# Layer 2's products stream the sum of mask and degree diagonal from one 16-bit tile

## Chip, core and metric

The kernel runs on one core of a Trainium2 chip. The metric is the device time of one execution in microseconds (us). TensorE (PE) multiplies matrices into PSUM, VectorE (DVE), ScalarE (ACT) and GpSimd (POOL) do the elementwise work, and SyncE issues the DMAs. The engines run on their own and are ordered by semaphores; each works through its own list of instructions in order.

## What is computed

Four graph layers with a residual and a layer norm each, on `x` (8 batches, 2048 nodes, 64 features) and a sparse, row-normalised adjacency matrix. The change concerns layer 2:

```python
adj_i = adj + jnp.eye(N, dtype=adj.dtype)
deg = jnp.sum(adj_i, axis=1, keepdims=True)
emb = jnp.einsum('bnf,hf->bnh', x, W) + b
agg = jnp.einsum('ij,bjh->bih', adj_i, emb) / deg
x = _layernorm(x + agg, axis=-1)
```

Every row of `adj` holds one value, 1 over its number of neighbours, so the kernel keeps `adj` as a 0/1 mask and scales rows afterwards. `adj + I` is then the mask plus a diagonal of the degrees, up to a scale of the rows.

## The kernel before

**Data.** `Bm` is the mask, transposed, in 8 bits, entries 0 or 64: 16 row tiles t of 128 nodes, 2048 columns. `dg` holds for each t a 128 x 128 tile in 16 bits with 64 times the degrees on its diagonal. `S` holds the activations as two 16-bit halves (high h = 0, low h = 1) for each t and each chunk c (two of the eight batches, 128 columns, c = 0 to 3). `stile(h, t, c)` is one 128 x 128 tile of it, the stationary operand of a matmul.

**The products of layer 2.** P0 to P15, with k = 4c + j: chunk c, output columns 512j to 512j + 511 (`block(j)`). `quarter` (L791, the matmuls are at L795) does four row tiles of a product, 8 matmuls of 512 columns; four quarters make 32. Behind the last quarter come 8 matmuls of 128 columns (L945) with `dg` as the streamed operand, for the four row tiles t = 4j to 4j + 3 whose nodes are those of the block. All 40 add into one PSUM bank; the last increments `s_p`. ACT then writes the high half of the result (step `E`, L1075) and DVE the low half (L1231), to free the bank.

```python
e.wait_ge(s_sl, 4 * c + q + 1)
quarter(e, o, c, j, q, False)
if q < 3:
    continue
for i in range(4):
    t = 4 * j + i
    for h in range(2):
        m = e.matmul(o[:, 128 * i:128 * i + 128], stile(h, t, c), dg[:, t, :], ...)
```

**Order.** The order of all steps is written out by hand in `middle_order` and `last_order`, the same list for every engine; each engine does its part of each step. P0 lies between the last steps `Z` of layer 0 (L925). `last_order` begins behind the last `Z`: a key y of `late` is a place in it, and P1's first half stands behind the keys up to 2, its second half behind key 3, P2's first half behind key 4, and so on. What stands at key 0, `sum(3)` among it, comes from `middle_order`.

The other steps that matter:

- `add` (POOL): joins the parts of a `Z` step into `X`. The last is that of the last `Z`.
- `chk` (ACT): counts a row tile of the mask, with `T3[:, 0:1024]` as its junk output; sixteen of them, the last behind the last `Z`.
- `bt` (POOL, L1773): an 8-bit addition over 512 columns, 64 of them, for mask combinations that layer 3 wants from about 670 us on.
- `sum(3)` (POOL): three additions for layer 1's mean over chunk 3, behind DVE's norm of layer 0 for that chunk (L1543).
- `split(c, j)` (ACT, POOL): writes the halves `S` of layer 1's result; `s_sl` counts them. A product of chunk c waits for them.
- `W(c, j)` (PE, L780 to L782, 12 matmuls of 128 columns; DVE, four additions into `X`): the product with the weights. Needs `E` of its product and a free PSUM bank.
- `rows` (DVE): constants of layer 3. `ovr` and `sgn` (ACT): two passes over a row tile of the adjacency, a check of the inputs.
- `v0`, `D`, `G`, `M`, `cut`, `mix`: layer 3. Its products `M` (L962) begin behind P15. The cuts `S1` and `S2` write `SUM`, whose first half lies in `T3[:, 0:1024]`.

Of the kernel before, what the change touches and what calls it, by code (L numbers as in the profile page):

```python
# [6 lines left out]
F16 = mybir.dt.float16  # L7
# [7 lines left out]
NT = 16  # L15
# [166 lines left out]
def last_order(after):  # L182
# [9 lines left out]
    def on(h, *steps):  # L192
        half.setdefault(h, []).extend(steps)

    for k in sorted(after):
        at(int(2 * k), *after[k])
    for c in range(NC):
# [110 lines left out]
def gnn_kernel(nc, x_in, at_in, a_in, embt_in, sm_in, bx_in, w0_in, a12_in, w0bb_in, out):  # L308
    ctx = ExitStack()
    with ctx:  # L310
# [72 lines left out]
        s_g, s_ut, s_uh, s_ul = (sem(f"s_{k}") for k in ("g", "ut", "uh", "ul"))  # L383
        s_gt, s_gh, s_gl = (sem(f"s_{k}") for k in ("gt", "gh", "gl"))
        s_f, s_y3 = sem("s_f"), sem("s_y3")
        s_bt = sem("s_bt")
        s_mx = sem("s_mx")
        s_over = sem("s_over")
        s_t2 = sem("s_t2")
# [60 lines left out]
        rowt = WZ[:, :, :, :].rearrange("p h k n -> p (h k n)")[:, 0:4096].bitcast(F32)  # L450
        junk = WZ[:, :, :, :].rearrange("p h k n -> p (h k n)")[:, 4096:6144]
        junk_counts = T3[:, 0:1024].bitcast(F16)
        RT = [flatR[:, 512 * k:512 * k + 512] for k in range(4)]
        UT = [flatR[:, 2048 + 512 * k:2560 + 512 * k] for k in range(4)]

# [332 lines left out]
            e.matmul(o, hat[:, 0, kd, :], T[:, c, 1, block(j)], start=False, stop=False, skip_group_check=on)  # L788
            return e.matmul(o, hat[:, 1, kd, :], T[:, c, 0, block(j)], start=False, stop=True, skip_group_check=on)  # L789

        def quarter(e, o, c, j, q, last=True):  # L791

            for t in range(4 * q, 4 * q + 4):
                for h in range(2):
                    m = e.matmul(o, stile(h, t, c), Bm[:, t, block(j)], start=(t == 0 and h == 0),  # L795
                                 stop=(last and t == NT - 1 and h == 1))
            return m

        def product1(e, v, q):
# [91 lines left out]
        def tensor_steps(e, steps):  # L891
            for step in steps:
                kind = step[0]
                if kind == "P1":
                    product1(e, *step[1:])
                elif kind == "dx":
                    pe_dx(e, step)
                elif kind == "t1":
                    pe_t1(e, step)
                elif kind == "P2":  # L900
                    product2(e, *step[1:])
                elif kind == "Z":
                    u, t = step[1:]
                    c, j = divmod(u, 4)
                    n4 = 4 * u + t
                    e.wait_ge(s_dx, u + 1)
                    e.wait_ge(s_u2, u + 1)
                    e.wait_ge(s_wlo, 1)
                    k0 = slice(128 * (4 * j + t), 128 * (4 * j + t) + 128)
                    halves = ([DX[:, c % 2, h, k0] for h in range(2)], [T[:, c, h, k0] for h in range(2)],  # L910
                              [U2[:, u % 3, h, 128 * t:128 * t + 128] for h in range(2)])
                    for g in range(2):
                        n = 2 * n4 + g
                        b0 = z_bank(n)
                        if n < 3:
                            for b in (b0, b0 + 1):
                                e.wait_ge(*z_first[b])
                        else:
                            e.wait_ge(s_za, 3 * (n - 2))
                        for i in range(9):  # L920
                            kd, part = divmod(i, 3)
                            zh, wh = ((0, 0), (0, 1), (1, 0))[part]
                            for q in range(2):
                                r = slice(64 * q, 64 * q + 64)
                                m = e.matmul(bank(b0 + q), halves[kd][zh][r, :], WZ[r, wh, kd, block(g)],  # L925
                                             start=(i == 0), stop=(i == 8))
                        m.then_inc(s_zp, 1)
                elif kind == "mean":
                    o = pe_aux(e, step)
                    e.wait_ge(s_sum, step[1] + 1)  # L930
                    e.matmul(o, ones[:, :], XS, start=True, stop=True).then_inc(s_mean, 1)
                elif kind == "P":
                    k, q = step[1:]
                    c, j = divmod(k, 4)
                    o = bank(product_bank(k))
                    if q == 0:
                        e.wait_ge(*product_free(k))
                    e.wait_ge(s_sl, 4 * c + q + 1)
                    quarter(e, o, c, j, q, False)
                    if q < 3:  # L940
                        continue
                    for i in range(4):
                        t = 4 * j + i
                        for h in range(2):
                            m = e.matmul(o[:, 128 * i:128 * i + 128], stile(h, t, c), dg[:, t, :], start=False,  # L945
                                         stop=(i == 3 and h == 1))
                    m.then_inc(s_p, 1)
                elif kind == "M":
                    n, s, q = step[1:]
                    jj = q // 2  # L950
                    what, by = SLOTS[s]
                    o, b = bank(pair_bank(n, s, jj)), mask(by, jj)
                    if q % 2 == 0:
                        e.wait_ge(*pair_free[step])
                    if n == 2 and by[0] == "T":
                        e.wait_ge(s_bt, NT * (1 + BT_ORDER.index(by)))
                    if jj == 0:
                        e.wait_ge(s_ul, CN["cut", n, q, what] + 1)
                    last = s in (1, 5, 6)
                    for t in range(4):  # L960
                        for h in range(2):
                            m = e.matmul(o, half_of(n, what, h, q % 2)[:, t, :], b[:, 4 * (q % 2) + t, :],  # L962
                                         start=(s in (0, 1, 3) and q % 2 == 0 and t == 0 and h == 0),
                                         stop=(not last and q % 2 == 1 and t == 3 and h == 1), skip_group_check=s not in (0, 1, 3))
                    if q % 2 == 1:
                        if last:
                            m = beside(e, o, *ending(n, s, jj), min(n // 2 - 1, 1), on=s > 1)
                        m.then_inc(s_p, 1)
                elif kind == "t22":
                    n, jj = step[1:]  # L970
                    beside(e, pe_aux(e, step), *ending(n, 4, jj), min(n // 2 - 1, 1), True).then_inc(s_t2, 1)
                elif kind == "total":
                    o = pe_aux(e, step)
                    e.wait_ge(s_cw, 1)
                    e.matmul(o[:, 0:2], ones[:, :], sums[:, 0, :], start=True, stop=True).then_inc(s_tot, 1)
                elif kind == "W":
                    c, j = step[1:]
                    o = pe_aux(e, step)
                    e.wait_ge(s_zl, 4 * c + j + 1)
                    e.wait_ge(s_hl, 1)  # L980
                    by_weight(e, o, c, j, 5).then_inc(s_w, 1)
                elif kind == "D":
                    c, j = step[1:]
                    o = pe_aux(e, step)
                    e.wait_ge(s_vl, 4 * c + j + 1)
                    by_diagonal(e, o, c, j).then_inc(s_d, 1)
                elif kind == "G":
                    p, c, j = step[1:]
                    o = pe_aux(e, step)
                    if p == 1:  # L990
                        e.wait_ge(s_hl, 3)
                        e.wait_ge(s_dl, 4 * c + j + 1)
                    else:
                        e.wait_ge(s_gl, place(p - 1, c, j) + 1)
                    by_weight(e, o, c, j, 2 + min(p - 1, 1)).then_inc(s_g, 1)
                elif kind == "F":
                    c, j = step[1:]
                    o = pe_aux(e, step)
                    e.wait_ge(s_gl, place(3, c, j) + 1)
                    by_weight(e, o, c, j, 4).then_inc(s_f, 1)  # L1000
# [72 lines left out]
        def scalar_steps(e, steps):  # L1073
# [3 lines left out]
            for step in steps:  # L1077
# [91 lines left out]
                elif kind == "cut":  # L1169
# [3 lines left out]
                    else:  # L1173
                        e.wait_ge(s_mx, MN["mix", n, jj, what] + 1)

                    if what in ("S1", "S2", "S3"):
                        if n > 2:
                            e.wait_ge(s_p, slot_done(n - 1, {"S2": 2, "S1": 3, "S3": 4}[what], 1))
                    elif n >= 4:
                        e.wait_ge(s_p, slot_done(n - 2, [x[0] for x in SLOTS].index(what), 1))  # L1180
                    else:
                        c, j = block_of(n, jj, "X21" if what == "S4" else what)
                        e.wait_ge(s_d, 4 * c + j + 1)
# [563 lines left out]
        def gpsimd_steps(e, steps, pc):  # L1747
# [3 lines left out]
            for step in steps:  # L1751
# [22 lines left out]
                elif kind == "add":  # L1774
# [12 lines left out]
                    e.wait_ge(s_acc[1], 5 * n4 + 5)  # L1787
                    add(v, v, Y[n4 % 3]).then_inc(s_add, 1)
                    e.wait_ge(s_add, n4 + 1)
                elif kind == "sum":  # L1790
                    c = step[1]
                    e.wait_ge(s_n[0], 4 * c + 2)
# [481 lines left out]
```

## Time and profile before

| | us |
|---|---|
| median of 3 runs | 1030.81 |
| lowest, highest run | 1030.46, 1031.53 |
| span of the profiled execution | 1029.5 |
| PE busy | 1009.6 (98%) |
| DVE busy | 678.8 (66%) |
| POOL busy | 553.4 (54%) |
| ACT busy | 457.4 (44%) |
| P0's last matmul to M's first | 519 to 654.6 |

The span runs from the first to the last instruction of the profiled execution. Times in the views count from its start. Matmuls overlap: one is shown for 0.38 us (512 columns) while they start 0.22 us apart, so the spacing of starts tells their cost. A busy time of PE is no proof of full speed.

### The profile page before, as it was taken

To read this page: it belongs to the slowest core of one execution; us is meant where nothing else is said; L and a number is where in the kernel's file an instruction comes from. 1 tells how busy PE (TensorE), PEld (TensorE's weight loads), DVE (VectorE), ACT (ScalarE), POOL (GpSimd) and SP (SyncE) were. 2 spreads that over 40 slices of the span, in tenths; PEclk is the share of its full clock that TensorE was granted. 3 is DMA by queue.
4 is the path that set the end of the run, shared out by engine and by line. 5 is a ranking of instruction groups with operands and counts; after the bars stand their busy time and mean duration, and the time that the engine had idled before them with its cause. 6 is when DMAs were issued, how large, how long until landed. Compare 5 with 4: busy or idle time off the path is not lost.

```text
span 1029.5 us, 18650 instructions
## 1 busy us (share of the span) xinstructions
PE 1009.6 (98%) x6854; PEld 485.6 (47%) x6854; DVE 678.8 (66%) x1683; ACT 457.4 (44%) x1109; POOL 553.4 (54%) x645
## 2 busy tenths in 40 slices
PE   7999999999999999999999999999999999999995
PEld 3445444444444444434445556555555545455553
DVE  3886565666566786578567767886663646657556
ACT  4632323453345445543543454432556655232632
POOL 0004487776658698879878465474534233323311
PEclk9999999999999999999999999999999999999998
DMA  9930000000000000000010111000033231000022
GB/s 375 402 136 1 1 1 2 1 2 1 1 1 2 1 2 2 1 2 1 1 42 1 41 42 42 2 1 1 3 122 108 98 123 42 4 2 21 21 62 62
DMA packets 14658, 45.65 MB, mean 44 GB/s; under 512 B 960, under 2 KB 9280, under 8 KB 10080
## 3 DMA queue, kind: packets, MB, share of 16 engines
q1 hardware_dynamic: 14560, 44.39, 11.7%
q8 instruction: 56, 0.92, 0.4%
q14 instruction: 42, 0.34, 0.1%
HBM read 40.19 MB, written 4.19 MB: 43 GB/s over the span
## 4 chain that ended last, share of the span: by engine, by line
PE 90%; DVE 6%; ACT 2%; issue 1%; POOL 0%; DMA 0%; SPq 0%; ACTq 0%; DVEq 0%; POOLq 0%
PE PS L962 28%; PE PS L925 23%; PE PS L795 22%; PE PS L847 5%; PE PS L780 2%; PE PS L781 2%; PE PS L782 2%; ACT WZ L1075 1%; DVE X L1543 1%; DVE X L1231 1%; PE PS L789 1%; PE PS L787 1%; PE PS L788 1%; DVE T L1231 1%; PE PS L770 1%
## 5 line engine op out<-in xcount | busy, mean ns | idle before, releaser
L795 PE MATMUL PS<-BW,S 128*128 128x512 fp8e4 x1280 | 290.7, 379 | 0.7 <-DVE R L1231 0.7
L1075 ACT ACTIVATE T<-PS,SM 128x128 f32<-128x128 f32 x384 | 113.2, 366 | 203.8 <-DVE X L1231 135.8
L925 PE MATMUL PS<-WZ,R 64*128 64x512 f16 x1536 | 197.8, 377 | 0.0
L795 PEld LDWEIGHTS PS<-BW,S 128*128 128x128 f16 x1280 | 120.2, 98 | 149.4 <-issue 16.6
L962 PE MATMUL PS<-BW,S 128*128 128x512 fp8e4 x768 | 173.1, 379 | 0.1
L1749 POOL TENSOR_TENSOR T<-T 128x128 f32<-128x128 f32 (+1 forms) x192 | 124.3, 647 | 79.8 <-ACT T L1075 61.8
L1231 DVE SCALAR_TENSOR_TENSOR X<-PS,SM,X 128x128 f32<-128x128 f32 x320 | 109.9, 344 | 76.0 <-PE PS L925 75.9
L925 PEld LDWEIGHTS PS<-WZ,R 64*128 64x128 f16 x1536 | 69.5, 94 | 102.6 <-issue 26.3
L962 PEld LDWEIGHTS PS<-BW,S 128*128 128x128 f16 x768 | 73.8, 98 | 83.4 <-issue 0.6
L962 PE MATMUL PS<-BW,T 128*128 128x512 fp8e4 x480 | 109.3, 379 | 0.0
L1749 POOL TENSOR_TENSOR S<-R,S 128x512 f16<-128x512 f32 (+1 forms) x46 | 52.5, 1148 | 103.9 <-ACT S L1075 103.9
L1231 DVE SCALAR_TENSOR_TENSOR T<-PS,SM,T 128x128 f32<-128x128 f32 x256 | 88.1, 344 | 24.9 <-PE PS L925 24.7
L925 PE MATMUL PS<-WZ,T 64*128 64x512 f16 x768 | 103.8, 376 | 0.0
L1749 POOL TENSOR_TENSOR T<-R,T 128x512 f16<-128x512 f32 x40 | 50.4, 1269 | 84.0 <-ACT T L1075 50.3
L1075 ACT ACTIVATE WZ<-WZ,ra 128x2048 f16<-128x2048 f32 (+1 forms) x32 | 63.9, 1996 | 41.8 <-DMA WZ<-a_in 41.7
L1231 DVE SCALAR_TENSOR_TENSOR R<-PS,cs,R 128x512 f32<-128x512 f32 x48 | 36.0, 750 | 64.9 <-PE PS L789 29.2
L1773 POOL TENSOR_TENSOR BW<-BW 128x512 fp8e4<-128x512 fp8e4 x64 | 70.9, 1113 | 2.7
L962 PEld LDWEIGHTS PS<-BW,T 128*128 128x128 f16 x480 | 46.3, 98 | 52.9
L1231 DVE SCALAR_TENSOR_TENSOR R<-PS,ra,R 128x128 f32<-128x128 f32 x176 | 48.6, 343 | 30.5 <-PE PS L782 17.5
L1749 POOL TENSOR_TENSOR X<-X,T 128x128 f32<-128x128 f32 x128 | 58.5, 457 | 10.0
L780 PE MATMUL PS<-hat,T 128*128 128x128 f16 x320 | 57.1, 219 | 3.4 <-DVE T L1231 2.5
L847 PE MATMUL PS<-BW,S 128*128 128x512 fp8e4 x240 | 54.8, 393 | 5.6 <-DVE BW L1228 5.6
(210 smaller groups left out, 1496.6 us busy)
## 6 DMA issues: line engine op xcount, KB each, us to landing
WZ<-a_in SPq DMA_DIRECT2D x16, 1024.0 KB, 4.8
BW<-at_in SPq DMA_DIRECT2D x8, 1024.0 KB, 18.9
R<-at_in SPq DMA_DIRECT2D x7, 1024.0 KB, 12.9
out<-X SPq DMA_DIRECT2D x16, 256.0 KB, 2.3
X<-x_in SPq DMA_DIRECT2D x3, 1024.0 KB, 20.6
T<-w_in SPq DMA_DIRECT2D x1, 1536.0 KB, 16.1
R<-at_in SPq DMA_DIRECT2D x2, 512.0 KB, 4.1
SM<-sm_in SPq DMA_DIRECT2D x1, 520.5 KB, 18.9
```

The source lines that it names most:

```text
L770: e.matmul(o[:, 128 * k:128 * k + 128], stile(0, t, c), dg[:, t, :], start=True, stop=False)
L780: e.matmul(ok, th, hat[:, 0, kind, :], start=True, stop=False)
L781: e.matmul(ok, tl, hat[:, 0, kind, :], start=False, stop=False)
L782: m = e.matmul(ok, th, hat[:, 1, kind, :], start=False, stop=True)
L795: m = e.matmul(o, stile(h, t, c), Bm[:, t, block(j)], start=(t == 0 and h == 0), stop=(last and t == NT - 1 and h == 1))
L847: e.matmul(bank(2 * c + j), stile(h, jt, c), Bm[:, jt, block(j)], start=(jt == 0 and h == 0), stop=False)
L925: m = e.matmul(bank(b0 + q), halves[kd][zh][r, :], WZ[r, wh, kd, block(g)], start=(i == 0), stop=(i == 8))
L962: m = e.matmul(o, half_of(n, what, h, q % 2)[:, t, :], b[:, 4 * (q % 2) + t, :], start=(s in (0, 1, 3) and q % 2 == 0 and t == 0 and h == ...
L1075: return e.activation(o, i, f, **kw)
L1231: return e.scalar_tensor_tensor(out=o, in0=a, scalar=s, in1=b, op0=f, op1=g)
L1749: return e.tensor_tensor(o, a, b, f)
L1773: e.tensor_tensor(o, a, b, f, saturate=False).then_inc(s_bt, 1)
```

## The change

The mask's diagonal 128 x 128 tiles and the tiles of `dg` are added into `dm`, 16 tiles of 128 x 128 in 16 bits, which lie in `T3[:, 0:1024]`. POOL does this in four new steps `dm` of four additions each, at keys 0, 2, 4 and 6 of `last_order`, for blocks 1, 2, 3 and 0. P1 to P15 no longer have matmuls against `dg`. Their own four row tiles are done last, by `own_rows`: around each diagonal tile the columns left and right of it come from the mask, the diagonal tile from `dm`. The other twelve row tiles go in the three quarters before. P0 is left as it was. PE waits for `s_dm` ahead of the own rows, and ACT waits for `s_p` ahead of the first `S1` cuts, which overwrite `dm`.

```diff
+    for y, b in ((0, 1), (2, 2), (4, 3), (6, 0)):
+        at(y, ("dm", b))
     for k in sorted(after):
         at(int(2 * k), *after[k])
...
+        DM_AT = (0, 2, 3, 1)
+        dm = T3[:, 0:1024].bitcast(F16).rearrange("p (b i n) -> p b i n", b=4, n=128)
...
-        def quarter(e, o, c, j, q, last=True):
+        def quarter(e, o, c, j, q, last=True, first=0):
...
-                    m = e.matmul(o, stile(h, t, c), Bm[:, t, block(j)], start=(t == 0 and h == 0),
+                    m = e.matmul(o, stile(h, t, c), Bm[:, t, block(j)], start=(t == first and h == 0),
...
+        def own_rows(e, o, c, j):
+
+            for i in range(4):
+                t, d = 4 * j + i, 128 * i
+                for h in range(2):
+                    last = i == 3 and h == 1
+                    if d:
+                        e.matmul(o[:, 0:d], stile(h, t, c), Bm[:, t, 512 * j:512 * j + d], start=False, stop=False)
+                    if d < 384:
+                        e.matmul(o[:, d + 128:512], stile(h, t, c), Bm[:, t, 512 * j + d + 128:512 * j + 512],
+                                 start=False, stop=False)
+                    m = e.matmul(o[:, d:d + 128], stile(h, t, c), dm[:, DM_AT[j], i, :], start=False, stop=last)
             return m
...
-                    e.wait_ge(s_sl, 4 * c + q + 1)
-                    quarter(e, o, c, j, q, False)
+                    if k == 0:
+                        e.wait_ge(s_sl, q + 1)
+                        quarter(e, o, c, j, q, False)
...
+                    others = [x for x in range(4) if x != j]
                     if q < 3:
+                        e.wait_ge(s_sl, 4 * c + others[q] + 1)
+                        quarter(e, o, c, j, others[q], False, 4 * others[0])
                         continue
...
+                    e.wait_ge(s_sl, 4 * c + j + 1)
+                    e.wait_ge(s_dm, (4, 1, 2, 3)[j])
+                    own_rows(e, o, c, j).then_inc(s_p, 1)
...
+                    if what == "S1" and n == 2:
+
+                        e.wait_ge(s_p, 14 + 2 * jj)
...
+                elif kind == "dm":
+                    b = step[1]
+                    e.wait_ge(s_cnt, NT)
+                    e.wait_ge(s_dg, NT)
+                    for i in range(4):
+                        t = 4 * b + i
+                        m = add(dm[:, DM_AT[b], i, :], dg[:, t, :], Bm[:, t, 128 * t:128 * t + 128])
+                    m.then_inc(s_dm, 1)
```

## Rows read from the trace of the kernel before

**Rows 1.** The page, the chain that ended last, as shares of the span.
```profile
PE 90%; DVE 6%; ACT 2%; issue 1%; POOL 0%; DMA 0%; SPq 0%; ACTq 0%; DVEq 0%; POOLq 0%
```

**Rows 2.** PE's groups by line, 523 to 654 us: count, busy, mean ns, idle before.
```profile
L795 PE MATMUL PS<-BW,S 128*128 128x512 fp8e4 x480 | 106.7, 379 | 0.0
L780 PE MATMUL PS<-hat,T 128*128 128x128 f16 x89 | 15.8, 219 | 0.9 <-DVE X L1231 0.9
```

**Rows 3.** PE's instructions in order of time, 523 to 607: start, duration, what.
```profile
523.27 7.08 PE L795 MATMUL PS<-BW,S 128*128 128x512 fp8e4 x32
530.19 0.61 PE L945 MATMUL PS<-dg,S 128*128 128x128 f16 x8
530.64 7.07 PE L795 MATMUL PS<-BW,S 128*128 128x512 fp8e4 x32
...
537.99 0.22 PE L780 MATMUL PS<-hat,T 128*128 128x128 f16 x1
...
538.66 7.07 PE L795 MATMUL PS<-BW,S 128*128 128x512 fp8e4 x32
...
606.61 0.23 PE L780 MATMUL PS<-hat,T 128*128 128x128 f16 x1 [0.90 <-DVE X L1231]
```

**Rows 4.** POOL's instructions in order of time, 529 to 560: start, duration, what.
```profile
529.04 1.10 POOL L1773 TENSOR_TENSOR BW<-BW 128x512 fp8e4<-128x512 fp8e4 x1
533.86 1.64 POOL L1749 TENSOR_TENSOR SM<-X 128x512 f32<-128x512 f32 x1 [3.72 <-DVE X L1543]
535.58 2.94 POOL L1749 TENSOR_TENSOR SM<-SM,X 128x512 f32<-128x512 f32 x2
...
559.36 1.21 POOL L1749 TENSOR_TENSOR S<-X,S 128x512 f16<-128x512 f32 x1 [2.18 <-ACT S L1075]
```

**Rows 5.** ACT's instructions in order of time, 527 to 654.
```profile
527.95 0.21 ACT L1075 ACTIVATION_READ_ACCUMULATOR T<-BW 128x1 f32 x1
...
546.22 0.60 ACT L1075 ACTIVATE T<-PS 128x512 f16<-128x512 f32 x1 [1.12 <-PE PS L945]
...
601.65 0.57 ACT L1075 ACTIVATE T<-PS 128x512 f16<-128x512 f32 x1
...
653.41 0.60 ACT L1075 ACTIVATE T<-PS 128x512 f16<-128x512 f32 x1 [2.08 <-PE PS L945]
```

**Rows 6.** POOL's groups by line and shape, whole span.
```profile
L1749 POOL TENSOR_TENSOR S<-R,S 128x128 f16<-128x128 f32 x4 | 1.7, 427 | 11.9 <-ACT S L1075 11.9
L1749 POOL TENSOR_TENSOR X<-X,T 128x128 f32<-128x128 f32 x128 | 58.5, 457 | 10.0
L1773 POOL TENSOR_TENSOR BW<-BW 128x512 fp8e4<-128x512 fp8e4 x64 | 70.9, 1113 | 2.7
```

**Rows 7.** The chain of waits from P3's end, in order of time: start, duration, what.
```profile
546.22 0.61 ACT T L1075
...
576.25 2.00 ACT WZ L1075 x2
...
605.95 0.61 DVE X L1231 x2
```

**Rows 8.** Busy times by stretch; PEclk is the granted clock as a share.
```profile
1021.00:1029.50 8.50, 0.00 (x0) 0.00 (x0) 4.93 (x14) 0.85 (x2) 2.08 (x2) 0.54 0.44 123
```

**Rows 9.** PE's instructions in order of time, at the kernel's start, at 367, at the end.
```profile
5.55 34.72 PE L847 MATMUL PS<-BW,S 128*128 128x512 fp8e4 x147 [5.55 <-DVE BW L1228]
...
7.66 1.91 PE L847 MATMUL PS<-BW,S 128*128 128x512 fp8e4 x4
...
11.83 1.46 PE L847 MATMUL PS<-BW,S 128*128 128x512 fp8e4 x6
...
367.40 0.23 PE L833 MATMUL PS<-i,T 128*128 128x128 f16 x1 [1.32 <-DVE R L1231]
...
367.85 1.89 PE L795 MATMUL PS<-BW,S 128*128 128x512 fp8e4 x8
...
1020.09 0.22 PE L780 MATMUL PS<-hat,T 128*128 128x128 f16 x1 [2.06 <-DVE T L1231]
```

More of the change, by code:

```diff
@@ L385, in gnn_kernel @@
         s_f, s_y3 = sem("s_f"), sem("s_y3")
-        s_bt = sem("s_bt")
+        s_bt, s_dm = sem("s_bt"), sem("s_dm")
         s_mx = sem("s_mx")
@@ L789, in beside @@
             return e.matmul(o, hat[:, 1, kd, :], T[:, c, 0, block(j)], start=False, stop=True, skip_group_check=on)
-        def quarter(e, o, c, j, q, last=True):
+        def quarter(e, o, c, j, q, last=True, first=0):
             for t in range(4 * q, 4 * q + 4):
                 for h in range(2):
-                    m = e.matmul(o, stile(h, t, c), Bm[:, t, block(j)], start=(t == 0 and h == 0),
+                    m = e.matmul(o, stile(h, t, c), Bm[:, t, block(j)], start=(t == first and h == 0),
                                  stop=(last and t == NT - 1 and h == 1))
+            return m
+        def own_rows(e, o, c, j):
[9 more added lines that the diff above has]
+                    m = e.matmul(o[:, d:d + 128], stile(h, t, c), dm[:, DM_AT[j], i, :], start=False, stop=last)
             return m
@@ L937, in tensor_steps @@
                         e.wait_ge(*product_free(k))
-                    e.wait_ge(s_sl, 4 * c + q + 1)
-                    quarter(e, o, c, j, q, False)
+                    if k == 0:
+                        e.wait_ge(s_sl, q + 1)
+                        quarter(e, o, c, j, q, False)
+                        if q < 3:
+                            continue
+                        for i in range(4):
+                            for h in range(2):
+                                m = e.matmul(o[:, 128 * i:128 * i + 128], stile(h, i, c), dg[:, i, :], start=False,
+                                             stop=(i == 3 and h == 1))
+                        m.then_inc(s_p, 1)
+                        continue
+                    others = [x for x in range(4) if x != j]
                     if q < 3:
+                        e.wait_ge(s_sl, 4 * c + others[q] + 1)
+                        quarter(e, o, c, j, others[q], False, 4 * others[0])
                         continue
[L942 to L947, printed above, removed]
+                    e.wait_ge(s_sl, 4 * c + j + 1)
+                    e.wait_ge(s_dm, (4, 1, 2, 3)[j])
+                    own_rows(e, o, c, j).then_inc(s_p, 1)
                 elif kind == "M":
@@ L1789, in gpsimd_steps @@
                     e.wait_ge(s_add, n4 + 1)
+                elif kind == "dm":
+                    b = step[1]
+                    e.wait_ge(s_cnt, NT)
+                    e.wait_ge(s_dg, NT)
+                    for i in range(4):
+                        t = 4 * b + i
+                        m = add(dm[:, DM_AT[b], i, :], dg[:, t, :], Bm[:, t, 128 * t:128 * t + 128])
+                    m.then_inc(s_dm, 1)
                 elif kind == "sum":
```

## Prediction

> **What bounds the kernel now.** I read the page's busy shares first: TensorE (PE) works 98% of the span, and the chain that ended last is PE for 90% of it [rows 1]. So two things can move the end: less PE work, or a new wait of PE. The stage in question is layer 2, the sixteen products P0 to P15, 519 to 654 us. The groups by line over 523 to 654 us hold P1 to P15: 480 matmuls of 512 columns, 32 for each product; behind them come 8 of 128 columns against `dg`, so 120 in all. In this stretch PE idles for 0.9 us, once, ahead of a weight product [rows 2]. The order of PE's work around the first products gives the spacings and the moments at which each product starts [rows 3].
>
> **What it removes and adds on PE.** 32 matmuls of 512 columns take 523.27 to 530.19, 6.92 us or 0.216 each; the 8 of 128 columns take 530.19 to 530.64, 0.45 us or 0.056 each [rows 3]. The line through both is 0.417 ns for a column and 2.4 ns for an instruction. Before, a product's four diagonal row tiles cost 8 x 0.216 + 8 x 0.056 = 2.17 us. After, each half (high and low) of them is 10 matmuls: four of 128 columns against `dm`, two each of 128, 256 and 384 columns against the mask. Both halves are 12 x 0.056 + 4 x 0.109 + 4 x 0.163 = 1.76 us. A product saves 0.417 us, and 15 products 6.26 us. P0 is as before. The short matmuls each load their own weights; a load is shown as 0.10 us long, but the 12 weight products between P2 and P3 (128 columns, all with loads) take 537.99 to 538.66, again 0.056 each [rows 3], so I take the loads as hidden. The Trainium skill ("TensorE: Matmul & The Clock Gate", section "Back-to-back issue gap") speaks against it: in a real kernel it gives about 81 ns for a pair of load and matmul at 128 columns. By that figure a product would save 0.32 us, not 0.42, and the sum below would end 0.8 us later. The rows of this kernel show 56 ns, and the measurement decides.
>
> **The new wait.** The own rows of P1 wait for `dm(1)`, four additions on GpSimd (POOL). PE reaches them 24 matmuls into P1: 523.27 + 24 x 0.2157 = 528.45. In POOL's order `dm(1)` stands behind the last `add` of layer 0 and the `bt` behind it, which runs 529.04 to 530.14 [rows 4]. The other thing it waits for, the last `chk` of ScalarE (ACT), is done at 528.16 [rows 5]. So `dm(1)` starts at 530.14, later than PE wants its result. No row shows an addition of 16 bits and 8 bits on 128 columns. The nearest are 0.43 us (16-bit output, 128 columns) and 0.46 us (32 bits, 128 columns) [rows 6]; 512 columns take 1.11 in 8 bits [rows 6] and 1.47 in 32 bits (the last two of `sum(3)`, 2.94) [rows 4], so 8 bits do not cost more. Back to back, a start is some 0.04 us before the end of the one before. The bounds are 0.38 and 0.49 us; I take 0.42, nearest to the 16-bit row. Four are 1.7 us, done at 531.8; with 0.1 us to wake, PE goes on at 531.9. **Wait 1: 3.45 us.** P1 ends at 533.66.
>
> `dm(2)` stands in POOL's order behind `sum(3)`, whose three additions wait for VectorE (DVE) until 533.86 and end at 538.52 [rows 4]; DVE's part of that comes from layer 0's norm and not from P1. `dm(2)` is done at 540.2. PE wants it at 533.66 + 5.18 = 538.84 and goes on at 540.3. **Wait 2: 1.45 us.** P2 ends at 542.06 (before 537.99) [rows 3]. `dm(3)` follows two `bt` (1.07 each) and is done near 544.1, PE wants it at 542.06 + 0.67 + 5.18 = 547.9: no wait. `dm(0)` is done near 550.5, PE wants it at about 555.5: no wait. The sixteen additions push back POOL's `bt` and `split` steps by up to 6 us; the `bt` are wanted after 654 only, and the first `split` of chunk 2 is wanted at P8, near 580, long after. P3 ends at 549.66 instead of 538.66 + 6.92 + 0.45 = 546.03, late by 3.45 + 1.45 - 3 x 0.417 = **3.65 us**.
>
> **Where that goes.** PE alone would win it back: 4.9 us of waits against 6.26 us saved. But P3's end starts a chain that is not PE's. ACT evicts P3 at 546.22 at once (it had idled 1.1 us for it), DVE follows, and from there the chain of waits runs over DVE (the `rows` constants), POOL, ACT (the two passes over a row tile, 2.0 us each, `ovr` and `sgn`) and DVE without a hole until 606.56, where PE's weight product W(2,1) waits for DVE to free its PSUM bank: the 0.90 us idle [rows 3, 5, 7]. The later evictions have no part in when this chain ends, as P4 to P10 are done before they are wanted: P9, for one, is evicted at 601.65 with no idle of ACT ahead of it [rows 5], so it was there first. So 3.65 us at P3 are 3.65 us at 606.6, and what P4 to P10 save is spent idling there. POOL's part of the chain, `split(2,3)`, is reached at 559.36 after 2.2 us idle [rows 4]; with the additions in front POOL would be free at about 559.3, so they hide there. After 606.6 PE is the limit again: ACT, for one, idles 2.1 us for P15 [rows 5], so the engines catch up, and P11 to P15 save 5 x 0.417 = 2.09 us. End: +3.65 - 2.09 = **+1.56 us**. The end of the kernel follows PE's last matmuls, so this passes through. The wait that the change adds ahead of the `S1` cuts costs nothing: in ACT's order these cuts stand behind the evictions of P14 and P15, which wait for the same products. The reordering of a product's quarters asks at the start of P8 and P12 for the second `split` of a chunk instead of the first; both stand at least two products ahead in POOL's order, so this costs nothing.
>
> The profiled execution spans 1029.5 us; the three runs have 1030.46 to 1031.53, median 1030.81, so some 1.3 us lie around the span, which the change does not touch. Forecast: 1030.81 + 1.56 = **1032.4 us**. With 0.38 to 0.49 us for an addition, both waits move, by 0.2 to 0.6 us together: 1031.9 to 1033.1 for this case.
>
> **Rivals.** (B) *The clock falls in wait 1.* At the end of the kernel PE idles 2.06 us, works 0.8 us, idles again, and the granted clock, 1.00 until then (2.4 GHz), means 0.54 over the last 8.5 us: it fell to 1.2 GHz soon after [rows 8, 9]. With the 1.32 us idle before 367.40 it did not: the 8 long matmuls behind it keep 0.216 us [rows 9]. 3.45 us of idle lie beyond both. After the idle start of the kernel matmuls are 0.426 us apart at 7.7 to 9.6 and 0.216 at 11.8 [rows 9]. PE's first matmul is at 5.55 [rows 9], so the half rate held PE back for 4 to 6 us, and 2 to 3 us were lost. Wait 2 would cover 1.45 us of that. Net 0 to 1.5 us, and a second fall at the idle of 606 would have no cover. I take +1.0: 1033.4 us, slower than before. It decides from the point where PE's idle at 528 is long enough to bring the fall. The Trainium skill ("TensorE: Matmul & The Clock Gate", section "What's actually happening") has the half rate as the default, which activity lifts; by that rule a wait like this one brings case B. The rows of the kernel's end agree.
>
> (C) *`dm(1)` is there in time* (POOL's order or my additions are wrong by 3.4 us). Then P3 is 1.25 us early, the chain too, and the end is -1.25 - 2.09 = -3.3: 1027.5 us. Against it: 529.04 is a recorded start. This also is the most that the change can give here.
>
> (D) *The chain from P3 to 606 gives way*, since a step that came last in the profile had others close behind it, or one of its long `issue` pieces shrinks. If all 3.65 us were taken up, W(2,1) would start at 606.61 as before, and the end is -2.09: 1028.7. Partly: anything up to the forecast.
>
> (E) *It does not do what it says*: the short matmuls are bound by their weight loads at 0.10 us. 12 x 0.042 us more make the own rows last 2.26 us, dearer than before; wait 2 shrinks to 0.95, and the end is near +5.1: 1035.9 us. The weight products' 0.056 us speak against it.
>
> **How the numbers follow.** Forecast 0.42, B 0.33, C 0.05, D 0.12, E 0.08. A difference of 0.2% (2.06 us, from 1028.75 to 1032.87) is about what a measurement tells from no change. Faster: C and a third of D, 0.09. Slower: E, most of B (0.27) and the forecast's upper end (0.06), 0.41. Within: 0.50. The range leaves out C, E, the lower part of D and the top of B: 1030.6 to 1034.2.
>
> **What would show it.** Right: PE idle near 528.5 for 3.4 us and near 538.9 for 1.4 us, both until a POOL addition; own rows in 1.76 us; ACT's eviction of P3 near 549.9; an idle of PE before W(2,1) that ends near 610; M starts 1.5 us later than now. Wrong: no idle at 528; W(2,1) at 606.6; spacings of 0.43 us after 532, which is B; own rows of over 2 us, which is E.

## The result, and the profile after

| | before | after |
|---|---|---|
| median (lowest, highest) of 13 runs, us | 1031.3 (1030.46, 1031.88) | 1032.86 (1031.51, 1033.86) |
| span of the profiled execution, us | 1029.5 | 1030.4 |

The ratio is 1.0016, 95% interval 1.0008 to 1.0023. The interval lies wholly above 1, so the changed kernel is slower, by about 1.6 us; that is less than the 0.2% which the prediction takes as telling from no change. The time forecast was 1032.4 us, in a range of 1030.6 to 1034.2. In a second set of runs (e8 below) it was 1.0019 (1.0009 to 1.0029).

PE's instructions in order of time in the changed kernel, around the own rows of P1 and P2 and at W(2,1) (start, duration, what, idle before and its releaser), which answer to [rows 3]:

```profile
522.73 5.35 PE L799 MATMUL PS<-BW,S 128*128 128x512 fp8e4 x24
531.20 0.32 PE L812 MATMUL PS<-BW,S 128*128 128x384 fp8e4 x1 [3.12 <-POOL T L1779]
...
532.61 0.31 PE L812 MATMUL PS<-BW,S 128*128 128x128 fp8e4 x1
532.72 0.31 PE L814 MATMUL PS<-T,S 128*128 128x128 f16 x1
...
533.68 6.29 PE L799 MATMUL PS<-BW,S 128*128 128x512 fp8e4 x24
539.80 0.33 PE L812 MATMUL PS<-BW,S 128*128 128x384 fp8e4 x1
...
541.56 0.22 PE L784 MATMUL PS<-hat,T 128*128 128x128 f16 x1
...
609.01 0.23 PE L784 MATMUL PS<-hat,T 128*128 128x128 f16 x1 [2.08 <-DVE X L1261]
```

Wait 1 is there: PE idles 3.12 us for `dm(1)`, and its first own row starts 3.29 us later than it would without a wait (3.45 in the forecast). The matmuls behind it start 0.11 us apart at 532.61 and 532.72, and P2's 24 long ones take 6.1 us and not 5.2: the clock has fallen. PE reaches P2's own rows at 539.80. `dm(2)` has been done since 539.41, so wait 2 does not show: the slow matmuls lasted longer than it would have. P2's own rows, at full clock, last from 539.80 to 541.56: 1.76 us, as worked out. The granted clock by stretch (the column behind the five engines; 1.00 is 2.4 GHz, 0.50 is 1.2 GHz) confirms it:

```profile
528.00:532.10 4.10, 0.98 (x12) 0.78 (x12) 2.16 (x8) 2.27 (x4) 2.97 (x6) 1.00 0.02 4
532.10:536.00 3.90, 3.90 (x19) 2.10 (x18) 3.90 (x5) 0.00 (x0) 2.63 (x2) 0.56 0.00 2
```

POOL's instructions, which answer to [rows 4]:

```profile
528.48 1.09 POOL L1803 TENSOR_TENSOR BW<-BW 128x512 fp8e4<-128x512 fp8e4 x1
529.53 1.51 POOL L1779 TENSOR_TENSOR T<-dg,BW 128x128 f16<-128x128 f16 x4
533.29 1.64 POOL L1779 TENSOR_TENSOR SM<-X 128x512 f32<-128x512 f32 x1 [2.24 <-DVE X L1573]
535.01 2.94 POOL L1779 TENSOR_TENSOR SM<-SM,X 128x512 f32<-128x512 f32 x2
537.90 1.51 POOL L1779 TENSOR_TENSOR T<-dg,BW 128x128 f16<-128x128 f16 x4
...
561.79 1.21 POOL L1779 TENSOR_TENSOR S<-X,S 128x512 f16<-128x512 f32 x1 [2.52 <-ACT S L1102]
```

`dm(1)` comes right behind the `bt`, `dm(2)` right behind `sum(3)`. Four additions take 1.51 us, 0.2 less than I took. ACT evicts P3 at once when it ends, as in [rows 5]:

```profile
549.36 0.60 ACT L1102 ACTIVATE T<-PS 128x512 f16<-128x512 f32 x1 [3.53 <-PE PS L814]
```

**Where the time went.** The same step in both traces, each counted from P1's first matmul (523.27 before, 522.73 after), so that differences of the kernel's first half drop out. The table is worked out from starts in the traces; the kernels of the later columns are those of the experiments.

| start of | before | after | e1 | e2 | e4 | e5 | e6 | e10 | e12 |
|---|---|---|---|---|---|---|---|---|---|
| W(0,1) on PE, P3's end | 546.01 | +3.70 | 0.00 | +2.03 | -1.25 | 0.00 | -1.25 | +3.49 | +3.49 |
| E(3) on ACT | 546.22 | +3.70 | +0.08 | +2.03 | -0.43 | +0.10 | -0.41 | +3.49 | +3.49 |
| E(4) on DVE | 557.27 | +2.98 | +0.68 | +2.58 | -0.28 | +0.68 | -0.25 | +3.04 | +3.04 |
| `addrow(3,0)` on POOL | 564.56 | +2.98 | +0.97 | +2.58 | -0.05 | +0.96 | -0.02 | +3.05 | +3.04 |
| W(2,1) on PE | 606.61 | +2.95 | +0.94 | +2.54 | -0.08 | +0.94 | -5.10 | +3.03 | -0.49 |
| P11 | 607.29 | +2.95 | +0.94 | +2.54 | -0.08 | +0.94 | -5.11 | +3.03 | -0.50 |
| layer 3's first product | 654.55 | +0.87 | -1.15 | +0.46 | -2.17 | -1.15 | -6.55 | +0.95 | -2.24 |

The column of after is the prediction's story: +3.7 at P3, carried by the other engines to W(2,1), then -2.08 over P11 to P15. The other columns have -2.08 or -2.09 there too, but for e6 and e12 (-1.44 and -1.74), where PE is held up by 0.64 and 0.34 us at W(2,3). Two things differ: the chain gave back 0.7 us between E(3) and E(4), and the medians lie above what the traces show. The experiments take them up.

Part of the spread of runs has nothing to do with layer 2: P1's first matmul, the zero of the table, starts at 522.43 us in e1's trace and at 523.63 in e2's, before anything in which these kernels differ. A median of eleven runs evens this out, a single trace does not.

### The profile page after: what moved, and what is told of

Same layout as the page of the kernel before. It is cut to its first block, busy times and chain, and to the rows that moved or that the text cites. A ratio compares the mean times of both kernels' runs of the same rounds, so it can differ in the third digit from the quotient of the medians.

```text
span 1030.4 us, 18807 instructions
## 1 busy us (share of the span) xinstructions
PE 1005.2 (98%) x6914; PEld 489.9 (48%) x6914; DVE 679.2 (66%) x1683; ACT 456.7 (44%) x1109; POOL 559.8 (54%) x661
## 4 chain that ended last, share of the span: by engine, by line
PE 89%; DVE 6%; ACT 2%; issue 1%; POOL 1%; DMA 0%; SPq 0%; ACTq 0%; POOLq 0%; DVEq 0%
PE PS L989 28%; PE PS L943 23%; PE PS L799 20%; PE PS L865 5%; PE PS L784 2%; PE PS L786 2%; PE PS L785 2%; DVE X L1261 1%; ACT WZ L1102 1%; DVE X L1573 1%; PE PS L793 1%; PE PS L791 1%; PE PS L792 1%; DVE T L1261 1%; PE PS L774 1%
## 5 line engine op out<-in xcount | busy, mean ns | idle before, releaser
L799 PE MATMUL PS<-BW,S 128*128 128x512 fp8e4 x1160 | 265.7, 380 | 0.7 <-DVE R L1261 0.7
L799 PEld LDWEIGHTS PS<-BW,S 128*128 128x128 f16 x1160 | 108.8, 98 | 136.1 <-issue 18.0
L989 PE MATMUL PS<-BW,S 128*128 128x512 fp8e4 x768 | 173.1, 379 | 0.0
L989 PEld LDWEIGHTS PS<-BW,S 128*128 128x128 f16 x768 | 73.8, 98 | 83.3 <-issue 0.5
L865 PE MATMUL PS<-BW,S 128*128 128x512 fp8e4 x240 | 54.0, 389 | 5.9 <-DVE BW L1258 5.9
```

The costliest lines, as they stand in the source:

```text
L865: e.matmul(bank(2 * c + j), stile(h, jt, c), Bm[:, jt, block(j)], start=(jt == 0 and h == 0), stop=False)
```

## The experiments

All ratios are against runs of the kernel before on the same chip, with the 95% interval; medians of before were 1031.08 (e1 to e4), 1031.26 (e5 to e8) and 1031.09 us (e9 to e12).

### e1: P1 to P3 as before

```diff
-                    if k == 0:
-                        e.wait_ge(s_sl, q + 1)
+                    if k < 4:
+                        e.wait_ge(s_sl, 4 * c + q + 1)
...
```

> P1 to P3 keep the 8 matmuls against dg as P0 does; P4 to P15 use dm. POOL still does its 16 additions at the same places. Theory of the prediction (two waits at P1 and P2, a chain of the other engines from P3's end to the weight product W(2,1), then PE's own pace): no wait of PE near 528 or 539, P3 ends when it ended before, W(2,1) starts where it did before (606.6), PE idles there for 0.9 + 7 x 0.417 less what it waits earlier, some 3 to 4 us, and the end is 5 x 0.417 = 2.1 us earlier than before. Rival (a saving on PE counts wherever it is made): 12 x 0.417 = 5.0 us earlier, no longer idle at W(2,1). Rival (own rows or the additions cost time in themselves): no earlier than before.

Measured: median 1033.15 us (1030.65 to 1034.16), ratio 1.0018 (1.0009 to 1.0027). In the trace no wait at P1 and P2, P3 on time, and idle that moved. PE's waits from 500 to 660 us (who for whom, total, times, longest):

```profile
PE PS L784 <- issue: 2.0, 1, 2.0
PE PS L784 <- DVE X L1261: 0.9, 1, 0.9
```

The first is ahead of W(2,0), at 594.58. The view names no releaser, but DVE's part of `E(8)`, which W(2,0) needs, ends at 594.48. In the kernel before nothing idled there. The savings of P4 to P10 are idled away, as claimed. But W(2,1) is 0.94 us late with no wait at all in front: the additions cost the chain something. And the median is 2.1 us above that of before, where I had expected 2.1 us below it; the trace, of the fastest of the eleven executions, is 0.4 us below. A fall of the clock shows here too:

```profile
592.50:595.80 3.30, 1.28 (x17) 0.99 (x16) 2.57 (x3) 0.63 (x2) 0.83 (x1) 1.00 0.00 0
595.80:599.20 3.40, 3.40 (x10) 1.22 (x8) 1.72 (x5) 3.40 (x5) 3.25 (x3) 0.50 0.00 0
599.20:606.70 7.50, 6.62 (x66) 4.50 (x65) 3.07 (x8) 5.73 (x11) 4.70 (x5) 1.00 0.41 142
```

### e2 and e3: dm(2) earlier, and wait 1 filled

e2 moves one step; e3 also lets PE work through wait 1.

```diff
-    for y, b in ((0, 1), (2, 2), (4, 3), (6, 0)):
+    for y, b in ((0, 1), (0, 2), (4, 3), (6, 0)):
...
+                    if k == 1:
+                        e.wait_ge(*product_free(2))
+                        for i in range(14):
+                            e.matmul(bank(product_bank(2)), stile(0, 0, c), Bm[:, 0, block(j)], start=True, stop=True)
                     e.wait_ge(s_dm, (4, 1, 2, 3)[j])
```

> The changed kernel with dm(2) moved up behind dm(1), ahead of sum(3), where POOL idled 2.2 us. Theory: wait 1 stays at 3.3 us from start to start, wait 2 goes. With the clock up P3 ends 3.3 - 1.25 = 2.0 us late and the kernel ends with 2.0 - 2.1 = 0 us against before. If PE's clock falls in wait 1, as in the changed kernel's profile (3.4 us at half rate, 1.7 us lost), nothing covers it now, and the end is +1.7 us. Rival (wait 1 alone sets P3's end, dm(2) was never late in earnest): the time of the changed kernel, +1.6 us, at either clock.

> As e2_dm2_up, and PE fills wait 1 with 14 matmuls of 512 columns into the bank of P2, whose result P2 overwrites (3.0 us of work that computes nothing). It tells the clock's part from the wait's: theory, no stretch at half rate behind 531, P3 2.0 us late, the end within 0.3 us of before in each run, 1.7 us less than those runs of e2 whose clock fell, and a narrower spread of runs. If the clock costs nothing: the same as e2.

Measured: e2 1031.9 us, 1.0008 (0.9999 to 1.0017); e3 1032.01 us, 1.0009 (1.0 to 1.0018). With wait 2 gone P3 is 2.03 us late, as worked out, so wait 2 did count, and the rival is out. W(2,1) is 2.54 us late, 0.5 more than P3, and layer 3 starts 0.46 us late and not on time; the median, +0.8 us, lies between the two cases of the theory. In e2's trace PE idled 3.12 us and the clock stayed up:

```profile
532.00:536.00 4.00, 3.90 (x30) 2.44 (x31) 3.86 (x8) 0.00 (x0) 2.54 (x5) 1.00 0.03 6
```

So an idle of 3.12 us brings the fall in one execution and not in another. e3 missed: no gain, and a spread of 3.4 us (1030.6 to 1034.04) in place of a narrow one. Its trace idles 0.9 us at W(2,0) and 2.1 us at W(2,1), and these idles were not filled. e3 says nothing on the clock's price at P1, only that a fall there is not what makes e3's spread.

### e4: dm(1) and dm(2) within layer 0

```diff
-    for y, b in ((0, 1), (2, 2), (4, 3), (6, 0)):
+    for y, b in ((0, 3), (2, 0)):
...
+    at(42, ("dm", 1))
+    at(58, ("dm", 2))
...
-        junk_counts = T3[:, 0:1024].bitcast(F16)
+        junk_counts = T3[:, 0:512].bitcast(F8)
...
-                    e.wait_ge(s_cnt, NT)
+                    if b in (3, 0):
+                        e.wait_ge(s_cnt, NT)
```

> dm(1) and dm(2) are done within layer 0 (behind the Z steps 42 and 58), dm(3) and dm(0) first in the last part; the junk output of chk is 8 bits wide, so that the upper half of T3[:, 0:1024] is free for them. Theory: no wait of PE for dm, P3 ends 1.25 us early, so does the chain to W(2,1), and the end is 1.25 + 2.1 = 3.3 us earlier than before: 0.997. Rival (every saving counts): 6.3 us earlier. Rival (POOL's additions within layer 0 delay PE's Z steps): less than 3.3 us, with idle of PE before 520.

Measured: 1029.64 us (1028.56 to 1031.09), ratio 0.9989 (0.998 to 0.9998): 1.4 us faster, not 3.3. P3 is 1.25 us early, but ACT begins `E(3)` only 0.43 us early: another of ACT's steps stands ahead of it, which leaves 0.43 us of the 1.12 us idle of [rows 5] to win. By W(2,1) the rest is gone too. PE now idles 2.2 us ahead of W(2,0), and the clock falls behind it (stretch 593.70 to 597.10):

```profile
593.70:597.10 3.40, 3.18 (x17) 2.00 (x18) 1.09 (x3) 2.59 (x5) 1.81 (x2) 0.50 0.00 0
```

The trace has -2.2 us at layer 3, the median -1.4.

### e5: only P11 to P15 changed

e1's edit with `k < 11` in place of `k < 4`.

> P1 to P10 keep the matmuls against dg, only P11 to P15 use dm. e1, with the same waits and P4 to P10 changed too, had one execution at 1030.65 us and most near 1033; in its trace PE idles 2.0 us ahead of W(2,0), which it did not before, and the clock falls there for 3.4 us. Theory: what P4 to P10 save ahead of the chain's end at W(2,1) is idled away and can only cost, by the clock; without it PE idles 0.9 us at W(2,1) as before, nothing ahead of W(2,0), the clock does not fall, and the end is 2.1 us earlier than before (ratio 0.998), some 4 us earlier than e1's median. Rival (the additions or own rows cost 2 us outside what the traces show): like e1, slower than before.

Measured: 1030.02 us (1029.57 to 1030.78), ratio 0.999 (0.9981 to 0.9999). Seven products fewer are changed than in e1, and it is 3.1 us faster. PE idles once, 1.7 us at W(2,1). The chain is as late as in e1 (+0.94), and the end is +0.94 - 2.09 = -1.15, with -1.2 measured. My -2.1 forgot what e1's trace had already shown, the 0.94 us.

Where do the 0.94 us come from? In e5's column 0.10 are there at E(3), 0.68 at E(4) and 0.96 at `addrow`. Between E(3) and E(4) three of DVE's instructions are longer than before: the addition behind E(3) by 0.19 us, `ra` by 0.13 and `bc` by 0.28. The four behind them take 4.37 us in both. `bc` and the last two of the four, before, then e5:

```profile
551.76 0.92 DVE L1223 TENSOR_SCALAR bc<-bc,cs 128x64 f32<-128x64 f32 x1
555.17 2.07 DVE L1224 TENSOR_SCALAR R<-c1row,cs 128x64 f32<-128x64 f32 x2
```

```profile
551.77 1.20 DVE L1253 TENSOR_SCALAR bc<-bc,cs 128x64 f32<-128x64 f32 x1
555.12 2.42 DVE L1254 TENSOR_SCALAR R<-c1row,cs 128x64 f32<-128x64 f32 x2
```

The last two in the changed kernel, together and the second by itself, and POOL's last work ahead of a gap:

```profile
558.31 1.36 DVE L1254 TENSOR_SCALAR R<-c1row,cs 128x64 f32<-128x64 f32 x2
559.36 0.31 DVE L1254 TENSOR_SCALAR R<-c1row,cs 128x64 f32<-128x64 f32 x1
557.13 2.14 POOL L1803 TENSOR_TENSOR BW<-BW 128x512 fp8e4<-128x512 fp8e4 x2
```

The same instruction on 64 columns takes 1.01 us while POOL adds, and 0.31 us once POOL has run dry at 559.27. That is the 0.7 us that the chain gave back. All fourteen traces agree: the second `R<-c1row,cs` takes 0.31 us in four of them (after, e8, e10, e12), where POOL is idle, and 1.01 to 1.31 in the ten others, where POOL works beside it. In e5 the additions shift what POOL does beside DVE, and `bc` and its neighbours grow; in the changed kernel the step falls so late that POOL is idle beside its end. That fits both signs; it is read from the traces and was not tried by an experiment.

### e6: e4 with ovr and sgn moved

```diff
-        y = 14 + 4 * it if it < 3 else 51 + (7 * (it - 3)) // 3
+        y = (27, 38, 45)[it] if it < 3 else 51 + (7 * (it - 3)) // 3
```

> As e4_dm_early, and the three pairs of passes ovr and sgn that ACT makes within the products (2.0 us each, two pairs of them in the chain to W(2,1)) come later, at the places 27, 38 and 45 in place of 14, 18 and 22. Theory: these passes are what makes W(2,0) and W(2,1) late, so their idle goes (3.3 us in e4), all 15 products count, the clock stays up there, and the end is 6.3 + 0.9 = up to 7.2 us earlier than before. Rival (another chain is close behind): the end stays near e4's, 1.4 to 3.3 us earlier than before.

Measured: 1024.6 us (1024.34 to 1025.07, 5 runs), ratio 0.9939 (0.9925 to 0.9952): 6.7 us faster than before, of the 7.2 expected at most, and some 8 us faster than the changed kernel. PE's waits from 500 to 660 us are down to one line, 0.5 us, and the spread to 0.7 us:

```profile
PE PS L786 <- issue: 0.5, 1, 0.5
```

### e7 and e8: e1 and the changed kernel once more

> The kernel of e1 once more, for a second trace: e1's was of its fastest execution. If the clock's falls make the spread, a slower execution shows a stretch at half rate that reaches past W(2,1) at 606.7 or a second one; if not, it shows all its extra time with the clock up.

> The changed kernel once more, for a second trace. Theory: PE waits at P1 until dm(1) (3.1 us idle), P3 ends 3.7 us late whether or not the clock fell, since the second wait covers the fall; a fall at W(2,1), where PE idles 2 us, would come on top with up to 1.7 us.

Measured: e7 1033.13 us, 1.0022 (1.0011 to 1.0032); e8 1033.22 us, 1.0019 (1.0009 to 1.0029). e7's trace was again of the fastest execution of its set, 1030.76 us. It has the same idles as e1, 2.0 and 2.1 us, and no fall of the clock:

```profile
606.82 0.23 PE L784 MATMUL PS<-hat,T 128*128 128x128 f16 x1 [2.08 <-DVE X L1261]
```

Thus a fall behind W(2,0) is covered: with it (e1) PE idles 0.88 us at W(2,1), without it 2.08, and P11 starts within 0.03 us of the same place. e8 shows wait 1, a fall right behind it, P3 at +3.72 and W(2,1) at +3.01: the first trace over again.

What the longer executions do is in no trace, but the mean granted clock of every execution is on record. e7's traced one has 0.997, without a fall; the seven longer ones, 1033.06 to 1034.11 us, all have 0.995. By estimate a fall of 3.41 us to half rate takes 0.0017 off this mean, and in traces without a fall in layer 2 it is 0.995 to 0.997, as the last stretch at half rate, at the kernel's end, is 6 to 10 us long. So 0.995 can be a fall or a long last stretch, and e7 is not decided by it; but 0.992 needs two falls. The changed kernel has five such executions of 21 (e8 and the first thirteen), and they took 1033.19 to 1034.3 us; its three executions at 0.996, which have hardly room for one, took 1032.17 to 1032.66. The clock's part in its spread is thus seen in executions that no trace shows. Where the second fall lies the mean does not tell.

### e9 and e10: the idles filled

e9 is e1 and e10 the changed kernel, with PE's waits filled by matmuls whose results are overwritten; e10 also has the 14 matmuls of e3.

```diff
                 elif kind == "W":
                     c, j = step[1:]
+                    if (c, j) in ((2, 0), (2, 1)):
+                        k = 10 + j
+                        e.wait_ge(*product_free(k))
+                        for i in range(8):
+                            e.matmul(bank(product_bank(k)), stile(0, 0, 2), Bm[:, 0, 0:512], start=True, stop=True)
```

> The kernel of e1, and PE does 8 matmuls of 512 columns that compute nothing (1.7 us) ahead of its waits at W(2,0) and at W(2,1), into the bank of the next product, which overwrites them. The moments at which the waits end do not change. Both traces of e1 (1030.65 and 1030.76 us) end as late as before's although its median is 2 us later; one had a covered fall of the clock, one none. Theory: in the other executions the clock falls in the idle at W(2,1), uncovered, 1.7 us. Then with the fill the median drops by 1.5 to 2 us to about 1031.2, and the spread with it. Rival (another cause that the traces do not hold): the median stays near 1033.

> The changed kernel with the fills of e9 and 14 such matmuls in wait 1. Theory: no fall of the clock anywhere in layer 2; the waits, P3's end (3.7 us late by wait 2 of 1.7 us) and W(2,1) (3 us late) stay as they are. The end is that of the change's traces, +0.9 to +1.3 us against before, in place of the median +1.6 to +1.9, with a narrower spread. Rival (the clock has no part in the median): +1.6 to +1.9.

Measured: e9 1030.05 us (1029.51 to 1030.7), ratio 0.9988 (0.9979 to 0.9997); e10 1031.78 us (1031.41 to 1032.37), ratio 1.0007 (0.9998 to 1.0016). Against before on the same chip, more work on PE made e1 3.1 us faster (1.5 to 2 expected) and the changed kernel 0.9 to 1.3 us (it ends at +0.7, a little under the +0.9 to +1.3 expected), and the spreads went from 3.5 to 1.2 and from 2.4 to 1.0 us. The places of the waits in the traces are the same (P11 at +0.96 in e9, +3.03 in e10). The mean granted clock of the changed kernel's first 13 executions averages 0.9940, that of e10's eleven 0.9965, and none of e10's is under 0.995. By estimate, from the 0.0017 above, the filling saves one and a half falls in an execution: the one in wait 1, of which all but 0.2 us is covered, and half a one without cover, 0.8 us; that makes 1.0 us. e10 shows the filling work in wait 1, and then, in e12's view, wait 2, which the fall had hidden:

```profile
528.22 3.19 PE L976 MATMUL PS<-BW,S 128*128 128x512 fp8e4 x14
```

```profile
PE PS L812 <- POOL T L1779: 4.4, 2, 3.1
```

(e12's two waits are not filled: 3.1 us at P1 and 1.3 at P2; e10's own is 1.35 at P2).

A single fall of 3.4 us at half rate can cost 1.7 us; e9 won 3.1. Part of the rest is lost in layer 3, ahead of its fifth product block, where PE's program tests a flag and jumps. At the jump every trace loses 0.2 to 0.7 us between two starts, e9's 0.67. e1 loses only 0.18 there, but nine matmuls further on, in the middle of a product, it stops once more. PE there in e1, then at the jump in e9:

```profile
892.73 2.10 PE L989 MATMUL PS<-BW,S 128*128 128x512 fp8e4 x9
895.99 1.25 PE L989 MATMUL PS<-BW,S 128*128 128x512 fp8e4 x5 [1.15 <-issue]
```

```profile
893.59 1.67 PE L989 MATMUL PS<-BW,S 128*128 128x512 fp8e4 x7 [0.51 <-POOL T L1784]
```

e7 has this second stop too, at the same matmul, 1.08 us long; no trace of another kernel has it. e1 and e7 are the same program, so it may go with the program; its cause is not shown. The flag has been set for 7 to 8 us when PE reaches the jump. Jump and stop together cost e1 0.8 us more than e9. That is 0.8 us of the 3.1, the clock up to 1.7, and some 0.6 us at least stay open. That the clock fell at W(2,1) in e1's longer executions is argued from the filling and seen in no trace.

### e11 and e12: ovr and sgn moved in the kernel before and in the changed one

e6's edit alone, in each.

> The kernel before with nothing changed but the places of ovr and sgn, as in e6. Theory: it wins the idle of 0.9 us at W(2,1) and no more: 0.9 us earlier than before. The rest of e6's 6.7 us is then the change's own, 5.8 of the 6.26 us worked out. Rival (moving the passes is what made e6 fast): 3 us or more earlier.

> The changed kernel as it is, waits and all, with ovr and sgn moved as in e6. Theory: the waits at P1 and P2 cost PE 3.3 and 1.7 us, but the chain behind P3 is 6 us shorter and no longer sets W(2,1), so P4 to P10 count too: 5.0 - 6.26 - 0.9 = 2.2 us earlier than before, up to 1 us less where the clock falls at P1 and wait 2 does not cover it. Rival (the waits are what decides, the chain behind them does not matter): as the changed kernel, 1.6 us later.

Measured: e11 1030.45 us (1029.44 to 1031.1), ratio 0.9993 (0.9984 to 1.0002), 0.6 us; e12 1029.08 us (1028.45 to 1030.0), ratio 0.9981 (0.9972 to 0.999), 2.0 us. The move by itself is worth under 1 us (0.9 expected). Under the change it is worth 3.6 to 4.0 us, each median taken against before on its chip, since all that P4 to P10 save had stopped at this chain. e12 keeps both waits and P3 at +3.49, yet layer 3 starts 2.24 us early: 3.49 - 5.00 (twelve products of 0.417) - 0.9 (the idle that stood before) = -2.4 is the sum of the terms.

## Why the prediction was right or wrong

**The saving of a product**: right, 0.417 us. Own rows last 1.76 us at full clock, and P11 to P15 save 2.08 us against 2.09. The Trainium skill's 81 ns for a pair at 128 columns ("TensorE: Matmul & The Clock Gate", "Back-to-back issue gap") does not hold here: 20 short matmuls of 2048 + 2048 columns take 1.76 us, what 2.4 ns each and 0.417 ns for a column give. Case E is out.

**The two waits**: right in kind and nearly in size. P3's end was worked out at +3.65; the traces have +3.70 and +3.72 with a fall of the clock and +3.49 without (e10, e12), as an addition takes 0.38 us, my lower end, and not 0.42. e2 shows wait 2 by itself: 2.03 late without it. The range was wrong in one point: `dm(2)` starts behind `sum(3)` whenever `dm(1)` ends, so a dearer `dm(1)` lengthens wait 1 and shortens wait 2 as much. Both together move by four additions, -0.16 to +0.28 us, and not by 0.2 to 0.6.

**The chain from P3 to W(2,1)**: right as a mechanism. e12 and e6 remove it and the savings of P4 to P10 appear; e1 and e5, which differ in just these products, have P11 at the same place. In size it was mis-sized by 0.7 us: I passed 3.65 through unchanged, and +2.95 arrived. This is the partial case D, by a cause I had not named, the DVE step that runs faster beside an idle POOL (read from the traces, not tried). Without a fall of the clock +3.49 became +3.03 (e10).

**"They hide there"**: wrong. I compared only when POOL is free for `split(2,3)`. e5 has no wait and the chain is 0.94 us late all the same. The additions shift POOL's other work, and DVE's instructions beside it grow. In the changed kernel this loss does not show, because the step comes later.

**Case B**: the fall came in both traces of the changed kernel, cost 1.7 us, and wait 2 covered all of it but 0.2 (P3 at +3.70 against +3.49), as said. The forecast itself has no price for the idle at W(2,1), 2.1 us where 0.9 stood before, though case B names a second fall there: filling the idles takes 0.9 to 1.3 us off the median. So the agreement of +1.56 with +1.56 us is luck, errors that cancel. Without falls the change costs +0.95 us by e10's trace and +0.7 by its median, 0.6 to 0.9 less than forecast: 0.16 by the additions and 0.45 by the chain. Falls bring the rest. The median is a blend of the forecast's case, D and B. The Trainium skill (same page, "What's actually happening") has the half rate as the default, which activity lifts. That agrees with e9 and e10, where work that computes nothing made the kernel faster.

**Case C's ceiling** of -3.3 us: wrong by its first term. Of 1.25 us that P3 gains, `E(3)` takes 0.43 and W(2,1) 0.08 (e4); with the -2.09 that is -2.2, and the median had -1.4.

## What to carry to other kernels

Before a saving on the busiest engine is multiplied by its count, find the next place where that engine waits for another: what is saved ahead of it is idled away there, and the chain that ends there is the first thing to shorten (one line moved: 3.6 to 4.0 us in e12, 5.2 in e6 against e4). A helper result that another engine makes must be placed by that engine's queue at the moment of need, which is one look at two timelines. And an idle that looks free can cost the clock: compare the spread of runs before and after, and their mean granted clock.

## What the runs showed of the hardware

- An idle of PE of 2.0 to 3.1 us dropped the clock from 2.4 to 1.2 GHz in some executions and not in others: 2.0 us in e1 and e7, which are one program, and 3.1 us in the changed kernel and in e12, which have the same wait. Where it fell, the half rate lasted 3.4 us.
- Work without a purpose in these idles lowered the median by 3.1 us (e9) and 0.9 to 1.3 us (e10), though PE waits for the same events.
- A DVE instruction on 64 columns takes 1.01 to 1.31 us while POOL works beside it (ten traces) and 0.31 us when POOL is idle (four traces).
- A tested jump costs PE 0.2 to 0.7 us between two starts, with the flag set 7 to 8 us before. In one program, in both of its traces (e1, e7), PE stops once more nine matmuls behind it, for 1.1 us.
